# Deformable convolution on Trainium2: a fourth product buffer, pool additions over whole thirds, and one reduction for two steps

## The reference

```python
om = conv3x3(x, w_off) + b_off             # 27 channels per pixel
off_y, off_x, mask = om[:, :9], om[:, 9:18], sigmoid(om[:, 18:])
py, px = off_y + row + ky, off_x + col + kx
sampled = bilinear(x, py, px) * mask       # 0 outside the image
out = einsum('bckhw,ock->bohw', sampled, w.reshape(O, C, 9)) + b
out = relu(batch_norm(out)) + x            # x: (8, 16, 64, 64), O = C = 16
```

## Time and profile before

| | |
|---|---|
| Median of 3 runs | 864.39 us (864.0 to 865.27) |
| Profiled execution, its own time | 861.69 us |
| Its span in the trace | 859.9 us |
| First product of the sampling stage starts | 322.09 us |
| Last reduction of the stage ends | 832.54 + 1.15 = 833.69 us |
| VectorE busy in the span | 719.1 us (84%) |
| TensorE, GpSimd, ScalarE busy | 692.2, 603.3, 584.7 us |

### The profile page before, as it was taken

How to read it: one execution, slowest core, us unless ns; L and a number is a source line. 1 busy time by engine, 2 the same in 40 slices (tenths; PEclk the granted TensorE clock), 3 DMA queues, 4 the chain that set the end, 5 groups by cost and what they waited for, 6 DMA issues and landing times.

```text
span 859.9 us, 30275 instructions
## 1 busy us (share of the span) xinstructions
PE 692.2 (80%) x12282; PEld 500.2 (58%) x12282; DVE 719.1 (84%) x935; ACT 584.7 (68%) x1089; POOL 603.3 (70%) x401
## 2 busy tenths in 40 slices
PE   5968888885999958888888788888878887777763
PEld 1325565554446647666766666667666666555542
DVE  3469999997322119999999999999999999999975
ACT  2646776774213239788788798888888988777714
POOL 3047888781410008898898998999999999989960
PEclk9989999998999979999999999999999999999976
DMA  4000000000481148555555555565466555555302
GB/s 164 1 0 2 1 0 0 0 0 0 112 204 27 21 106 207 140 156 151 141 140 162 145 158 147 143 166 161 120 167 166 141 157 152 160 146 156 96 4 98
DMA packets 29937, 90.69 MB, mean 105 GB/s; under 512 B 10622, under 2 KB 10750, under 8 KB 29566
## 3 DMA queue, kind: packets, MB, share of 16 engines
q1 hardware_dynamic: 26672, 88.12, 38.3%
q10 hardware_dynamic: 3150, 0.88, 0.5%
HBM read 79.01 MB, written 3.28 MB: 96 GB/s over the span
## 4 chain that ended last, share of the span: by engine, by line
PE 40%; DVE 39%; issue 15%; ACT 2%; DMA 1%; POOL 1%; DVEq 1%; ACTq 0%; SPq 0%; POOLq 0%
PE PS L1128 40%; DVE region L767 19%; DVE region L779 9%; DVE region L645 2%; DVE region L601 2%; DVE region L605 1%; DVE region L620 1%; DVE region L607 1%; PE PS L1210 1%; DVE region L602 1%; DMA region<-px_scratch 1%; ACT region L874 0%; DVE region L575 0%; DVE region L561 0%; DMA cst<-in_consts 0%
## 5 line engine op out<-in xcount | busy, mean ns | idle before, releaser
L1128 PE MATMUL PS<-region 64*64 64x144 f32 (+3 forms) x10112 | 456.4, 292 | 112.6 <-issue 81.2
L1128 PEld LDWEIGHTS PS<-region 64*64 64x64 f32 (+1 forms) x10112 | 342.2, 134 | 219.9 <-issue 198.3
L767 DVE TENSOR_TENSOR region<-PS,region 128x864 f32<-128x864 f32 x384 | 381.2, 1046 | 12.4 <-PE PS L1128 12.3
L509 POOL TENSOR_TENSOR region<-region 128x768 f32<-128x768 f32 x128 | 202.4, 1581 | 67.5 <-DVE region L767 67.5
L513 POOL TENSOR_TENSOR region<-region 128x864 f32<-128x864 f32 x128 | 224.0, 1750 | 18.7 <-POOL region L509 0.4
L1006 ACT ACTIVATE region<-region 128x1152 f32<-128x1152 f32 x128 | 149.2, 1165 | 34.3 <-PE PS L1128 30.6
L1003 ACT ACTIVATE region<-region,cst 128x1152 f32<-128x1152 f32 x128 | 159.2, 1244 | 7.7 <-DMA region<-px_scratch 6.3
L779 DVE TENSOR_REDUCE region<-region 128x32 f32<-128x960 f32 x128 | 145.9, 1140 | 1.5 <-POOL region L513 1.5
L1037 ACT ACTIVATE region<-x,cst (+2 forms) x288 | 86.7, 414 | 0.0
L1128 PE MATMUL PS<-wg,xp 64*64 64x144 f32 x1024 | 82.6, 286 | 5.0 <-issue 4.9
L432 POOL TENSOR_TENSOR region<-region,cst 128x1024 f32<-128x1024 f32 x32 | 61.4, 1917 | 31.4 <-PE PS L1203 25.3
(11 more groups left out here) (118 smaller groups left out, 590.6 us busy)
## 6 DMA issues: line engine op xcount, KB each, us to landing
region<-px_scratch SPq DMA_DIRECT2D x256, 288.0 KB, 4.3
out<-region SPq DMA_DIRECT2D x4, 512.0 KB, 3.0
region<-xp SPq DMA_DIRECT2D x8, 140.2 KB, 2.9
region<-xp SPq DMA_DIRECT2D x8, 140.1 KB, 2.8
region<-xp SPq DMA_DIRECT2D x8, 140.0 KB, 2.9
cst<-in_consts SPq DMA_DIRECT2D x1, 1104.0 KB, 8.6
region<-xp SPq DMA_DIRECT2D x8, 132.0 KB, 2.7
region<-xp SPq DMA_DIRECT2D x8, 131.9 KB, 2.7
```

The costliest lines, as they stand in the source:

```text
L509: pool.tensor_tensor(two_rows[:, :, :, 0:2 * THIRD - KEEP], two_rows[:, :, :, 0:2 * THIRD - KEEP], two_rows[:, :, :, KEEP:2 * THIRD], ALU. ...
L767: v.tensor_tensor(uu[:, 2 * u:2 * u + 2, :, THIRD * t:THIRD * (t + 1)], PS[:, 2 * t:2 * t + 2, 0:THIRD * C].rearrange("p h (a o) -> p h o ...
L1128: return nc.tensor.matmul(o, l, r, start=start, stop=stop)
```

## The change

The first addition of GpSimd takes the whole second third (864 elements in place of 768), so that 27 terms and not 30 are left for VectorE. VectorE sums two steps in one reduction: after the products of every odd step n from 3 on, it reduces steps n-3 and n-2 together, 4 rows x 16 channels x 27 terms = 1728 elements in, 64 out. It waits for the fold of step n-2, and raises `os_ready` by 2. `UB` is 4, and the fourth buffer lies over `two` and `bd`, which move from tiles of their own into `region2`.

```diff
@@ -38,10 +38,9 @@
 GR = 2
 STEPS, SPC = H // 2, RPC // 2
 THIRD = KK // 3 * NR
-KEEP = THIRD + 3
 ROUNDS = (3, 3, 2)
 XPARTS = ((0, 1), (1, 2), (2, 4), (4, NCH))
-UB = 3
+UB = 4
 XS = (H + 2) * (W + 2)
 
 
@@ -125,11 +124,8 @@
         cst = sb("cst", [P, NCC])
         bcol = sb("bcol", [P, 1])
         xp = sb("xp", [P, (H + 2) * (W + 2)])
-        bd = sb("bd", [P, 6, P])
         MEAN, WQ, WK, WV, PO, SA = range(6)
         woff = sb("woff", [P, 3, W])
-        two = sb("two", [P, 2, 2 * CH])
-        rs = two[:, 0, CH:CH + P * 2].rearrange("p (h a) -> p h a", h=2)
         small = sb("small", [P, 64])
         wg = sb("wg", [P, PAIRS, KK * C])
 
@@ -171,7 +167,12 @@
         img = cut(IR * KK * C)
         bns = aw[:, 0:6 * NCH]
         mk = cut(H * PAIRS * KK)
-        cut2 = cutter("region2", 2 * 2 * KK * W + UB * 2 * NA * C)
+        cut2 = cutter("region2", 2 * 2 * KK * W + (UB - 1) * 2 * NA * C + 4 * CH + 6 * P)
+        cut2(2 * 2 * KK * W + (UB - 1) * 2 * NA * C)
+        two = cut2(4 * CH).rearrange("p (u k) -> p u k", u=2)
+        bd = cut2(6 * P).rearrange("p (s k) -> p s k", s=6)
+        rs = two[:, 0, CH:CH + P * 2].rearrange("p (h a) -> p h a", h=2)
+        cut2(None)
         kb = cut2(2 * 2 * B * K1).rearrange("p (u w k) -> p u w k", u=2, w=2)
         kvb = cut2(2 * 2 * 2 * B * K2).rearrange("p (u w t k) -> p u w t k", u=2, w=2, t=2)
         ee = cut2(2 * B * (K1 + K2)).rearrange("p (u k) -> p u k", u=2)
@@ -506,8 +507,8 @@
                     if n % SPC == 2 and s < PAIRS * NCH:
                         modulate(s, s // NCH, s % NCH)
                     pool.wait_ge(u_ready, 3 * n + 5)
-                    pool.tensor_tensor(two_rows[:, :, :, 0:2 * THIRD - KEEP], two_rows[:, :, :, 0:2 * THIRD - KEEP],
-                                       two_rows[:, :, :, KEEP:2 * THIRD], ALU.add).then_inc(half_ready, 1)
+                    pool.tensor_tensor(two_rows[:, :, :, 0:THIRD], two_rows[:, :, :, 0:THIRD],
+                                       two_rows[:, :, :, THIRD:2 * THIRD], ALU.add).then_inc(half_ready, 1)
                     pool.wait_ge(u_ready, 3 * n + 6)
                     pool.wait_ge(half_ready, n + 1)
                     pool.tensor_tensor(two_rows[:, :, :, 0:THIRD], two_rows[:, :, :, 0:THIRD],
@@ -769,14 +770,14 @@
                         aw4[:, bass.ds(line, 2), 3 * t:3 * t + 3, :].rearrange("p h k j -> p h (k j)").unsqueeze(2).to_broadcast([P, 2, C, THIRD]),
                         ALU.mult).then_inc(u_ready, 1)
 
-            def totals(line, g):
-                return os4[:, bass.ds(line, 2), bass.ds(g, 1), :].rearrange("p y g o -> p y (g o)")
+            def totals(line, g, rows=2):
+                return os4[:, bass.ds(line, rows), bass.ds(g, 1), :].rearrange("p y g o -> p y (g o)")
 
             def interpolate_all():
                 def add(n):
                     b = 2 * (n % UB)
-                    dve.wait_ge(fold_ready, done(n))
-                    v.tensor_reduce(totals(2 * (n % STEPS), n // STEPS), uu[:, b:b + 2, :, 0:KEEP], AX.X, ALU.add).then_inc(os_ready, 1)
+                    dve.wait_ge(fold_ready, done(n + 1))
+                    v.tensor_reduce(totals(2 * (n % STEPS), n // STEPS, 4), uu[:, b:b + 4, :, 0:THIRD], AX.X, ALU.add).then_inc(os_ready, 2)
 
                 for n in range(PAIRS * STEPS):
                     if n % SPC == 0:
@@ -784,9 +785,9 @@
                     if n >= UB:
                         dve.wait_ge(os_ready, n + 3 - UB)
                     products(n, 2 * (n % STEPS), n % UB)
-                    if n > 0:
-                        add(n - 1)
-                add(PAIRS * STEPS - 1)
+                    if n >= 3 and n % 2 == 1:
+                        add(n - 3)
+                add(PAIRS * STEPS - 2)
 
             def interpolate(p, g, band):
                 dve.wait_ge(aw_ready, p * NCH + NCH + LAST + 1)
```

## The result

The changed kernel takes 895.19 us, median of 4 runs (892.54 to 900.03), against 864.19 (861.3 to 865.27, 4 runs): ratio 1.037, 95% interval 1.031 to 1.043. It is slower by about 31 us where 6 us less were forecast.

A forecast was written before the change was run, and what follows sets the result against it. VectorE bounds the kernel, and GpSimd would after the change: 501.0 us of work from 324.60, then the last reduction, end the stage at 827.60 against 833.69. Gain 6.1 us off 864.39: 858.3, range 855.0 to 864.0.

The forecast's parts named there:

- What bounds the kernel now: Stage of 128 steps: VectorE sets the pace at 3.95 us a step, GpSimd right behind, 15.02 against 15.8 in four.
- The change on VectorE: Paired reduction: 1.93 us, then 0.04 before the next product; two steps cost 7.75 us, at most 7.81, against 7.90.
- The change on GpSimd: Longer first addition: 1.750 us, pitch 1.896; four steps and a mask 15.69 us, so GpSimd becomes the bound.
- No waits of GpSimd: Within the stage: GpSimd, 6 us behind VectorE from the outset, never waits; its last fold ends at 825.64.
- (a): VectorE's product waits more than 0.10 us behind the reduction just ahead; at 0.2, 862.1 us; chance 0.14.
- (b): GpSimd's longer addition costs more than the slope: at 2.03 ns an element 861.6 us; chance 0.09.
- (c): GpSimd's 26.4 us of waits for VectorE stay: 884.7 us, with half of them 871.5; chance 0.08.
- (d): TensorE not ready where six products adjoin: a wait like 0.31 us in each pair gives 871.7 us; chance 0.07.
- Faster, 0.79: Whole kernel: chance 0.79 of measuring faster than before, against 0.08 for the same and 0.13 for slower.

The follow-up runs named there:

- e9: Changed kernel's whole thirds and four buffers, but first addition's operands exchanged, one reduction a step, GpSimd's additions staggered by a step: 853.26 us against 861.09, ratio 0.990.
- e1: Kernel before plus 48 lone GpSimd additions behind its last fold, distances and row pitches varied: 864 elements at pitch 81 last 1.73 to 1.79 or 2.05 to 2.08 us.
- e5: Changed kernel with the two operands of GpSimd's first addition exchanged: 858.84 us, ratio 0.996 to the kernel before.
- e8: Kernel before with 29 terms kept in place of 30, first addition 800 elements at distance 29: 857.82 us, ratio 0.995.
- e4: Changed kernel with the old fold: first addition 768 elements at distance 30, paired reduction of 1920: 870.32 us, ratio 1.011 to the kernel before.
- e6: More lone additions as in e1, with operand order, result place and row start varied: unbroken 864 elements last 2.00 or 1.71 us by distance.

## Why the prediction was wrong, by its own steps

**What bounds the kernel now** held, with VectorE at 3.95 us a step and GpSimd right behind.

**The change on VectorE** held to about 0.02 us in each term: reduction 1.951 (forecast 1.93), the gap behind it 0.06 on average (0.04, bounds up to 0.10), six products 5.80 (5.78). A pair is 7.80 and not 7.75, which alone would be 3 us over the stage. In the trace of before there was nothing like it, and the nearest rows served. The Trainium skill (VectorE: DVE Perf Modes, The DRAIN you can't avoid) found for copies that the semaphore costs nothing extra. The runs here differ: the product behind the reduction starts 0.03 to 0.10 us after its end, and without the wait (e9, 564.23 to 565.19 with a reduction of 1.04) 0.08 before it. The prediction took that section of the Trainium skill to rule out any overlap; the section also says that a next instruction which is not held starts earlier, and with that the 0.08 agrees.

**The change on GpSimd** is the step that failed, at its first number: "The second has that size and pattern already and lasts 1.750 on average, the smaller 1.581: 0.169 us for 96 elements, 1.76 ns each." The size was the same, the pattern was not: L513 reads its second operand at distance 54, the new addition at 27. Two errors sit in the term. The small one: L509 lies at distance 30, L513 at 54, and the slope between them mixed two forms (864 elements last 1.79 at 30 and 1.73 at 54 in e1). By e5 the longer addition in a fast form lasts 1.786, 0.205 over 1.581, in place of 0.169: 128 x 0.036 = 4.6 us. The large one: in the form that the change has it lasts 2.079, another 0.293: 128 x 0.293 = 37.5 us. Together the forecast's -6.1 becomes -6.1 + 4.6 + 37.5 = +36.0 us for the stage; the profile shows +35.4. The `KEEP` = 30 of the kernel before put its addition at a fast distance; the upper bound of the step, 2.03 ns an element from L513, came from a fast form too and so bounded nothing. And with the addition at 1.750 the 6.1 us would still not have come whole. In e5 the way from GpSimd's first addition to the stage's end is 835.91 - 328.61 = 507.3 us, and VectorE waits for GpSimd for 2.1 of them; so by an estimate it can't fall below 505.2, which is 3.9 us less than before's 509.1.

**No waits of GpSimd** held: the backlog is 7 us from the outset (the fold of step 3 ends at 345.35, the last product of step 3 at 338.33), and behind the first step nothing is waited for.

**The rivals.** (a) fell: the gaps behind a reduction are 0.10 us at most, but for one of 0.44 and the wait at the end. (b) named the right term, with a price less than a tenth of what it took (3.3 of 42 us). The Trainium skill (GPSIMD Engine Reference, Elementwise — side-by-side cycle accounting) gives about 2.6 cycles an element, 2.17 ns at 1.2 GHz by an estimate; the runs agree for the cost of one element more, 2.19 ns in e8, where my slope said 1.76. By that estimate the first addition would last 1.789, as e5's does (1.786). That number of the Trainium skill was right where I had set it aside, and it still says nothing of the 0.293. (c) fell. (d) came true in part: over 322 to 834 us TensorE's granted clock is 0.94 in the changed kernel and 0.96 in e5, before 0.99, and products wait for TensorE in 18 short waits, 5.9 us behind 330 us, where 0.8 us of slack had been counted at the full clock. Here that is hidden behind GpSimd; in e4 it is seen.

**Faster, 0.79**, rested on one row taken for another. With the operands exchanged the same change is 0.4% faster, too little to call the forecast of 6 us right even then.

## What to carry to other kernels

Before a number is taken over from "an instruction of the same size", compare its operands' places too, not only the elements and the engine: here one constant, or the order of the two operands of a sum, moves an addition by 16% and the kernel by 4%. When an engine stands at 95% of the pace of the one that is to be relieved, price the relief on both, and probe the new form of the instruction alone first. And a wait for the instruction just ahead costs on either engine (0.11 to 0.19 us here); staggering two chains by one step takes it away.

## What the runs showed of the hardware

- GpSimd's two-input float32 addition in SBUF has two rates by the distance of its operands: second minus first, in elements, modulo 4. 1 or 2: 1.70 to 1.79 us for 864 elements; 3 or 0: 2.00 to 2.08, alone (e1, e6); 2.079 and 1.786 in the kernel (after, e5). Row pitch, start and the place of the result don't change the class in what was tried.
- VectorE and GpSimd slow each other when both read two operands from SBUF. In e1 the lone additions met VectorE's last residual sums, which read both inputs from SBUF. Four of these took 4.63 us before (the second fence), here 10.45, and an addition beside them 2.92 where the same form lasts 2.06 in the second round:

```profile
859.92 10.45 DVE L990 TENSOR_TENSOR region<-region,xp  x4 [1.74 <-ACT region L1268]
```

```profile
851.44 4.63 DVE L844 TENSOR_TENSOR region<-region,xp  x4 [1.74 <-ACT region L1122]
```

```profile
860.37 2.92 POOL L552 TENSOR_TENSOR region<-region 128x864 f32<-128x864 f32 x1
```

The Trainium skill (SBUF — State Buffer, Who interferes with whom) has it that a `tensor_tensor` of VectorE with both inputs in SBUF contends with GpSimd's reads, and one blocks the other. The runs agree: the additions start 3.0 us apart there, a little less than one of each behind the other (2.06 + 1.16 = 3.22). In e6 a fast addition beside the same sums lasts 2.57 in place of 1.70. The products of the sampling stage, with one input in PSUM, last no longer beside GpSimd's additions (1.046 on average) than ahead of the first of them (1.06), and GpSimd's second addition is at 1.75 beside them and 1.73 alone.
